# Groups of 4, 6 and 6 batches in place of 5, 5 and 6 in a fused block of routed attention and feed-forward experts

## What is computed

```
h = layernorm(x) * (1 + ca) + sa                      # scale and shift of each batch
scores = softmax(h @ gate_w.T); rw, sel = top_k(scores, 2)
x_sorted = rows of h (each token twice) sorted by (batch, expert)
q, k, v  = x_sorted @ q_w, @ k_w[expert], @ v_w[expert]; feature maps on q and k
o = linear attention over the rows of one (batch, expert) segment, at most 256 rows, 8 heads of 16
out = sum over the token's two rows of rw * o, normalised per head, @ o_w.T
x = x + ga * out
x = x + gb * experts(layernorm(x) * (1 + cb) + sb)
```

## Time and profile before

| | us |
|---|---|
| median of 3 runs | 1198.78 |
| lowest, highest | 1197.69, 1201.34 |
| the profiled execution, its own time | 1199.79 |
| its span, first to last instruction | 1198.1 |

### The profile page before, as it was taken

The page is one execution under the profiler, slowest core; times in us unless marked ns, Lnnn a source line. Parts: engine busy times, 40 slices in busy tenths (PEclk is TensorE's granted clock), DMA queues, the critical chain, the costliest instruction groups (busy, mean ns, idle before and its releaser), DMA issues.

```text
span 1198.1 us, 26036 instructions
## 1 busy us (share of the span) xinstructions
PE 1054.6 (88%) x8950; PEld 768.7 (64%) x8950; DVE 888.9 (74%) x2067; ACT 652.9 (54%) x1596; POOL 510.5 (43%) x464
## 2 busy tenths in 40 slices
PE   4776588999998978999899898988998899899997
PEld 3554356666665756666666666766776677677774
DVE  3875467799975566787778977888788877786774
ACT  2432244545543545666666565666667566555664
POOL 2207613231224354212222125766886654455552
PEclk9786779999988989999999999999999999999999
DMA  8972323332332333222222215312332323235330
GB/s 233 401 313 88 106 79 99 94 110 87 99 94 87 93 93 94 72 70 64 68 68 68 60 47 170 93 50 70 109 106 69 88 82 95 66 87 152 80 88 18
DMA packets 81134, 123.08 MB, mean 103 GB/s; under 512 B 8944, under 2 KB 63728, under 8 KB 76912
## 3 DMA queue, kind: packets, MB, share of 16 engines
q1 hardware_dynamic: 70768, 96.24, 26.5%
q0 software_dynamic: 10240, 25.18, 6.8%
HBM read 70.27 MB, written 51.12 MB: 101 GB/s over the span
## 4 chain that ended last, share of the span: by engine, by line
PE 57%; DVE 23%; issue 7%; ACT 7%; another core or an unknown queue 5%; DMA 0%; SPq 0%; POOL 0%; DVEq 0%; ACTq 0%; POOLq 0%
PE wide L1417 7%; PE bank L1392 6%; PE bank L1477 6%; PE bank L1677 6%; PE wide L1667 6%; PE bank L1667 6%; PE bank L1461 3%; DVE epp L1753 3%; DVE kvw L1760 2%; DVE att L1519 2%; PE bank L1469 2%; PE bank L1379 2%; PE bank L970 2%; PE bank L1406 2%
## 5 line engine op out<-in xcount | busy, mean ns | idle before, releaser
L1632 POOL TENSOR_TENSOR kvw<-kvw,hq 128x512 f32<-128x512 f32 x128 | 172.6, 1348 | 152.5 <-ACT kvw L1720 152.2
L1519 DVE SCALAR_TENSOR_TENSOR att<-reach,endrel,wide 128x1024 f32<-128x1024 f32 x152 | 194.6, 1280 | 53.4 <-PE wide L1417 30.9
L255 POOL DMA_INDIRECT routed_rows<-hq,idxs x128 | 128.2, 1002 | 233.8 <-DVE att L1519 125.0
L892 POOL DMA_INDIRECT gst<-attended_rows,idxs x128 | 134.6, 1051 | 217.2 <-DVE att L1519 111.5
L1753 DVE TENSOR_TENSOR epp<-kvw,epp 128x512 fp32r<-128x512 f32 x160 | 134.4, 840 | 87.0 <-ACT epp L1728 84.8
L1677 PE MATMUL bank<-epp,w2p 128*128 128x512 f32 x480 | 164.1, 451 | 11.2 <-DVE epp L1753 11.2
L1728 ACT ACTIVATE epp<-kvw 128x512 fp32r<-128x512 f32 x160 | 100.7, 629 | 82.0 <-DVE kvw L1760 77.6
L1667 PE MATMUL bank<-hp,w1p 128*128 128x512 f32 x480 | 138.8, 398 | 0.0
L1667 PE MATMUL wide<-hp,w3p 128*128 128x512 f32 x480 | 137.1, 394 | 0.0
L1417 PE MATMUL wide<-turned,kx 32*128 32x128 f32 x2432 | 116.9, 304 | 22.5 <-DVE att L1519 17.6
L1392 PE MATMUL bank<-kvw,turned 128*128 x304 | 132.2, 517 | 4.3 <-ACT turned L1282 1.6
(11 more groups left out here) (267 smaller groups left out, 1891.6 us busy)
## 6 DMA issues: line engine op xcount, KB each, us to landing
hq<-weight_rows SPq DMA_DIRECT2D x16, 2048.0 KB
rows<-routed_rows SPq DMA_DIRECT2D x76, 256.0 KB
routed_rows<-zero SPq DMA_DIRECT2D x2, 6144.0 KB, 27.0
attended_rows<-ob SPq DMA_DIRECT2D x76, 128.0 KB
routed_rows<-zero SPq DMA_DIRECT2D x1, 7168.0 KB, 46.7
out<-fin SPq DMA_DIRECT2D x16, 256.0 KB, 2.3
routed_rows<-hq,idxs POOLq DMA_INDIRECT x128
gst<-attended_rows,idxs POOLq DMA_INDIRECT x128
```

The source lines that it names most:

```text
L255: pool.indirect_dma_start(hs[s], bass.IndirectOffsetOnAxis(idxs[:, t, k:k + 1], 0), hq[:, t, :], None, bounds_check=BLOCKS[s] * P - 1, oob ...
L892: pool.indirect_dma_start(gst[:, u, k, :], None, orow[s], bass.IndirectOffsetOnAxis(idxs[:, t, k % TOPA:k % TOPA + 1], 0), bounds_check=BL ...
L1519: dve.scalar_tensor_tensor(out=att[:, n % 2, :, :], in0=reach[:, :, :].rearrange("p a c -> p (a c)").unsqueeze(1) .to_broadcast([P, 4, 2 * ...
L1632: pool.tensor_tensor(g, g, rows_of(1 - b % 2, n, n + 1), ALU.mult).then_inc(s_eu, 1)
```

## The change

`SUPER` becomes (4, 6, 6). The groups then have 40, 56 and 56 blocks, again 152 in all. Group 0 has 32 scatters and group 1 has 48. `COUNT`, the step that counts group 0, goes from 7 to 6; group 0's table has two chunks in place of three, so that three DVE instructions of stage one go and three come in group 1's table, whose start goes from turn 20 to turn 17. `BASES` and `SEGMENTS` go one turn earlier. `J1` is written with 38 in place of 30 and stays at 78.

```
-SUPER = (5, 5, 6)
+SUPER = (4, 6, 6)
...
-        CHUNKS = (3, 3, 4)
+        CHUNKS = (2, 4, 4)
...
-        COUNT = 7
-        CHOOSE, COUNTS, BASES, SEGMENTS = 1, (8,), 12, 16
-        TABLE = {1: 20, 2: 34}
+        COUNT = 6
+        CHOOSE, COUNTS, BASES, SEGMENTS = 1, (8,), 11, 15
+        TABLE = {1: 17, 2: 34}
...
-                table(dve, 0, 12)
+                table(dve, 0, 9)
...
-                elif i == COUNT + 6:
-                    for part in range(9, 12):
-                        table(dve, 0, part)
-                elif i == COUNT + 7:
+                elif i == COUNT + 8:
                     for part in range(3):
                         choose(dve, 1, 2, part)
-                elif i == COUNT + 8:
+                elif i == COUNT + 9:
...
-        J1 = [C0[1] + 30 + PERIOD * b for b in range(NB)]
+        J1 = [C0[1] + 38 + PERIOD * b for b in range(NB)]
```

More of the change, by code:

```diff
@@ L784, in routing_vector @@
                                                AX.X, ALU.add))
-                elif i == 5:
+                elif i == 4:
                     for part in range(3):
                         choose(dve, 0, 1, part)
-                elif i == 6:
+                elif i == 5:
                     for part in range(3, 7):
```

## The result

The changed kernel takes **1182.28 us** (median of 4 runs, 1180.06 to 1186.6), the kernel before 1198.24 on the same chip (4 runs): a ratio of 0.9897, with a 95% interval from 0.9864 to 0.9931. It is 1% faster. Two later measurements of the same two kernels, in two other sessions, gave 0.9951 [0.9918, 0.9983] and 0.9902 [0.987, 0.9934].

What follows compares the result with a forecast made beforehand. The prediction took the chain of waits as the bound, with PE carrying 57% and POOL none. Its terms, -8 + 0.8 + 24 + 0 - 6.9 - 3.0 + 1.5 = +8.4, gave 1207 us on the median's footing, range 1191 to 1222.

Steps and rivals of the forecast that it cites:

- Sixteen more doubles: +24: Attention, group 1: turns with two scatters rise from five to 21, each costing 1.5 us, so 24 us more.
- The low end of the bounds, 16 × 0.9 = 14: Attention, group 1: lower bound for sixteen more two-scatter turns, as a block with a full DVE takes up part of the delay.
- turn 17's double with 0.3: Attention, group 1: one of the five two-scatter turns before the change, with only 0.3 us over a usual block.
- Its mechanism: Stage one and attention: PE's signals reach others late beside back-to-back scatters; in attention ACT waits 2.16 us instead of some 1.1.
- POOL's scatters start every 1.28 us whatever DVE does: Stage one and attention: scatters keep this pace even across DVE instructions reading two SBUF operands; ACT, waiting for PE, is late.
- Stage one, -8 + 0.8: Before attention: eight fewer scatters save 7 us, a dropped table chunk 1; counting the larger group 1 adds 0.8.
- The rival that called for the second one to vanish: Stage one's second slow stretch does not come (-15 - 1), two-scatter turns cost 0.9 us each: 1190 us, chance 21%.
- their count alone does not set the end: Stage one: scatters end 4 us before PE's last turning; their count sets how long late signals last.
- Group 2, -6.9 and -3.0: Attention: turns 47, 52 and 57 no longer doubled, 6.9 us less; five fewer scatters from turn 60 on, 3.0 less.
- The 0.6 for a scatter beside gathers: Attention from turn 60 on: 16 us over the pace of gathers alone, 0.6 us for a scatter.
- Turns without scatters 0: Attention: turns 27 to 33 lose single scatters and 34 to 41 gain them; single against none costs 0.
- DVE's table parts +1.5: Attention: three table parts move onto turns 17 to 19 and cost 0.5 us each, 1.5 in all.

Runs made afterwards that it cites:

- a_odd: The changed kernel with group 2's 48 scatters sent as 24 pairs in the odd turns 35 to 81: 1207.13 us, ratio 1.0057.
- a_even: The changed kernel with group 2's 48 scatters sent as 24 pairs in the even turns 34 to 80: 1217.31 us, ratio 1.0123.
- c_run: The changed kernel with group 2's 24 pairs of scatters in 24 turns in a row, 34 to 57: 1198.66 us, ratio 0.9989.
- after_third: The changed kernel itself, measured and traced once more in one of the two sessions that ran everything 5% faster: 1122.0 us, ratio 0.9902.
- c_gap: The changed kernel with two short POOL fills ahead of the second scatter of a turn in attention: 1181.87 us, ratio 0.9855.
- b_less8: The kernel before without the last 8 of group 0's 40 scatters in stage one: 1187.62 us, ratio 0.9933.
- b_half: The kernel before with group 0's 40 scatters moving half of each row's numbers, into another DRAM tensor: 1194.99 us, ratio 0.9998.
- b_line34: The kernel before with only group 2's scatters spread from turn 34 on, one each turn: 1185.36 us, ratio 0.99.
- a_line42: The changed kernel with group 2's scatters back on their old line, from turn 42 on: 1202.96 us, ratio 1.0013.

## Why the prediction was wrong, step by step

**The step that failed is "Sixteen more doubles: +24".** It took the mean excess of five pairs that stand alone, 1.5 us, and multiplied it by 16. For lone pairs the price was near to right (1.6 in before as reckoned below, 0.9 to 1.0 in a_odd and 1.2 to 1.45 in a_even). It does not carry over to pairs in each turn, because the block behind a slow one is free then: 0.97 each in c_run. To price it in this kernel, take the trace of after_third as what blocks 0 to 33 need when nothing is late, 109.4 us, and 109.0 for the five pairs of before. The changed kernel's 127.8 is 18.4 above, 0.87 for each of 21 pairs; before's 117.1 is 8.1 above, 1.6 for each of five. The change did not add 16 pairs at 1.5; it turned five dear ones into 21 cheap ones, +10.3 us where +24 was forecast. The low end of the bounds, 16 × 0.9 = 14, was taken as a floor and was not one: it too multiplied the price of a lone pair. The row that should have warned was in the prediction's own list, turn 17's double with 0.3. An average over unlike events is no unit price.

**Its mechanism stood.** ACT acts late on PE's signals beside scatters 1.28 us apart, with the releaser unnamed (25% of the stretch's chain), and most of that goes when the second scatter of a turn starts 2.12 us after the first (c_gap, 6%). Blocks 2 to 25 took 4.02 us on average, between the 4.3 that was to confirm the doubles and the 3.5 that was to refute them. The prediction set this against the Trainium skill, "SBUF — State Buffer", section "Who interferes with whom", by which PE and ACT never wait on anyone. That rule is about the ports to SBUF. It has nothing on a signal that is late, so ACT's wait neither agrees with it nor breaks it, and to price a second scatter at nothing by it was more than it says. Why the signals are late is open. b_half excludes the bytes, c_gap shows that the place of the second scatter matters; no run changed what the signals themselves pass through.

**One reading was too strong.** "POOL's scatters start every 1.28 us whatever DVE does" holds for most of them. Of before's 40 scatters in stage one six took 1.05 to 1.55 us in place of 0.97, and five of these end within 0.02 us of the end of a DVE instruction, as this one does:

```profile
101.36 1.55 POOL L255 DMA_INDIRECT routed_rows<-hq,idxs  x1 [0.30 <-issue]
...
102.10 0.82 DVE L386 TENSOR_REDUCE wfull<-work 128x16 f32<-128x640 f32 x1
```

POOL does wait beside DVE, then, but 2 us in all.

**Stage one, -8 + 0.8.** Measured -9.6 and -7.5 in two traces of after, -9.6 for the middle one of nine traces of its stage one, and -8.4 by b_less8 for the eight scatters alone. The term holds, and so does its way: less of the late stretch, both stretches still there. The rival that called for the second one to vanish is refuted in these sessions. Its own condition, however, was met: it decides from where a double costs less than about 1 us, and an added one came to 10.3 / 16 = 0.64. The sign was that rival's, and the mechanism wasn't. In the two last sessions the first stage did gain about what it had asked for, 12 to 17 us, because there POOL's queue is what ends last, a case that the prediction had ruled out by "their count alone does not set the end".

**Group 2, -6.9 and -3.0.** These were about right. Blocks 41 to 59 gave -8.3 and -8.0 against the trace of before, and blocks 60 to 81 -6.8 and -2.6; but the trace of before is slow in the first stretch, 67.7 us where four other traces with the same scatters have 65.8, and in the second such traces run from 97.7 to 102.0 us and those of the even line from 94.0 to 99.2. Against the means of such traces the terms are -6.3 and -3.6. Measured alone, by b_line34, both are worth 10.7 us. The 0.6 for a scatter beside gathers was too low (0.8 to 1.0 in c_run): its base was the pace of blocks that only gather later on, 3.85 us, and with the scatters gone those 22 blocks take 3.5.

**The small terms.** Turns without scatters 0: +0.5 and +1.0. DVE's table parts +1.5: where nothing is late, blocks 0 to 33 differ by 0.4 between the kernels. The first stretch of gathers, expected the same, is so within 1 us.

With 10.7 in place of 25.5 for blocks 0 to 33 the sum of the forecast would have been -6.4, 1192 us, a ratio of 0.9947. The 10.7 is read from the result, so this tests the other terms only. The second measurement, 0.9951, is where that corrected sum ends; the first, 0.9897, is 6 us lower, and no term accounts for that: it is the difference between two sessions of one kernel.

**What stays open:** why PE's signals come late; whether gaps would gain in the kernel before or beside the gathers, since both kernels that asked it met the sessions without lateness; whether c_gap's gain is one of distance; and how much of its 12 us over the changed kernel is the scatter between runs, as the changed kernel's own two ratios, 0.9897 and 0.9951, differ by half a per cent. The 10.7 us in the traces lie in just the stretch that the gaps touch.

## What to carry to other kernels

Before multiplying the price of an event by a new count, look whether the block behind it pays or gets something back, and take the price from a place where events stand as densely as they will. Spread indirect DMAs of POOL evenly, one to a turn: an even line for group 2 was worth 10.7 us here. Where two must share a turn, try some 2 us between them: that was worth 10.7 us in blocks 0 to 25, in the one session that tested it where signals are late. Change one part at a time: the new groups alone gained nothing in these sessions (a_line42), and one line of the change nearly all (b_line34). Find out with a trace which of two late things sets a stage's end, since here it was PE in four sessions and POOL's queue in two. Before reading a term from two traces, see how far two traces of one program lie apart: 9 us in stage one here.

## What the runs showed of the hardware that was not expected

- **The same kernel took 1196 to 1199 us in four sessions and 1133 to 1135 in two.** The 5% lie only in stretches with indirect DMAs on POOL: blocks 60 to 81 took 94.0 us in after and 71.0 in after_third, blocks 100 to 150 198.2 and 183.6, while the rest after block 150, without any, took 462.3 and 462.2. It isn't the chip alone: the chip recorded as number 3 gave 1196.03 in one session and 1135.17 in a later one. What else differs the runs don't tell.
- **A scatter's cost to others doesn't depend on its bytes** (b_half: 0.9998), but on what is issued beside it: with the second of a turn 1.28 us behind the first a slow block has 1.9 us too much (4.98 against 3.07), with 2.12 us 1.0 (4.08 against 3.08).
- **The even or odd turn seems to matter**: 1.2 against 0.9 us for a lone pair over blocks 34 to 59, in one trace each; the intervals of the two totals overlap. The kernel's work alternates with a period of two blocks (ACT's L1314 is issued once for two), but what in it decides was not tried.
